# A transformer block on one core: three operations in another place in the rows of the loop, and the products of the last row spread anew over its slots

## The reference

```
xn  = (x - mean) / sqrt(var + 1e-5)
q,k,v = xn @ w_qkv.T + b_qkv                   # 16 heads of 32
att = softmax(q k.T / sqrt(32), causal) v
ffn = (silu(xn gate_w.T * gate_s) * (xn up_w.T * up_s)) @ down_w.T * down_s    # width 1408
out = x + att @ w_out.T + b_out + ffn
```

## Time and profile before

| | |
|---|---|
| median of 3 runs | 1941.37 us (1941.12 to 1942.3) |
| the profiled execution: its own time / its span in the trace | 1944.31 / 1942.6 us |
| PE busy | 1898.3 us, 98% |
| PE weight loads (beside PE) | 919.1 us, 47% |
| DVE / ACT / POOL busy | 1333.2 / 1294.1 / 1376.0 us (69 / 67 / 71%) |
| DMA packets | 840163, 267.93 MB |
| granted clock of TensorE, mean | 0.999 |

### The profile page before, as it was taken

The page is one execution under the profiler, slowest core; times in us unless marked ns, Lnnn a source line. Parts: engine busy times, 40 slices in busy tenths (PEclk is TensorE's granted clock), DMA queues, the critical chain, the costliest instruction groups (busy, mean ns, idle before and its releaser), DMA issues.

```text
span 1942.6 us, 48936 instructions
## 1 busy us (share of the span) xinstructions
PE 1898.3 (98%) x15875; PEld 919.1 (47%) x15875; DVE 1333.2 (69%) x3912; ACT 1294.1 (67%) x2315; POOL 1376.0 (71%) x1105
## 2 busy tenths in 40 slices
PE   5999999999999999999999999999999999999998
PEld 2444444444444444444444444444444444444443
DVE  8886766767666676766767666676766767667664
ACT  4876676666666676676766666676666766666574
POOL 1596687866678676687866778676687866778665
PEclk9999999999999999999999999999999999999999
DMA  9259777686876859777686876859678695876766
GB/s 341 47 93 161 145 121 150 116 152 130 151 144 110 160 104 162 137 122 150 115 153 129 152 145 109 158 103 166 135 122 148 114 156 126 150 147 112 132 131 120
DMA packets 840163, 267.93 MB, mean 138 GB/s; under 512 B 812976, under 2 KB 812976, under 8 KB 839344
## 3 DMA queue, kind: packets, MB, share of 16 engines
q1 hardware_dynamic: 839984, 265.15, 72.3%
HBM read 46.94 MB, written 16.78 MB: 33 GB/s over the span
## 4 chain that ended last, share of the span: by engine, by line
PE 72%; POOL 9%; issue 5%; DVE 5%; DMA 4%; SPq 3%; ACT 1%; DVEq 0%; POOLq 0%; ACTq 0%
PE ps L601 72%; POOL phl L1381 3%; POOL region_b L1338 3%; DMA p_t<-phl 3%; SPq L507 2%; DMA memory<-down 1%; POOL memory L1376 1%; DVE p L1268 1%; DVE memory L1059 1%; POOL rstd L1334 1%; SPq L587 1%; SPq L589 0%; DVE hidden_tmp L1201 0%; POOL region_a L1343 0%; POOL o_hl L1386 0%
## 5 line engine op out<-in xcount | busy, mean ns | idle before, releaser
L601 PE MATMUL ps<-x_t,memory 128*128 128x512 f16 x4376 | 994.8, 379 | 5.2 <-DVE qk L1151 2.0
L1381 POOL TENSOR_TENSOR phl<-p,phl 128x1024 f16<-128x1024 f32 x320 | 683.0, 2134 | 381.6 <-ACT phl L987 381.4
L977 ACT ACTIVATE p<-p,nmax 128x384 f32<-128x384 f32 (+3 forms) x1024 | 529.7, 557 | 275.9 <-DVE nmax L1268 256.7
L601 PEld LDWEIGHTS ps<-x_t,memory 128*128 128x128 f16 x4376 | 405.0, 97 | 494.0 <-issue 36.1
L1268 DVE CUSTOM_DVE_ANT_0 p<-ps,causal,cst 128x384 f32<-128x384 f32 (+3 forms) x1024 | 515.0, 546 | 98.2 <-PE ps L601 78.1
L987 ACT CAST phl<-p 128x1024 f16<-128x1024 f32 x320 | 334.1, 1044 | 40.1 <-DMA p_t<-phl 24.2
L601 PE MATMUL ps<-memory 128*128 128x512 f16 (+1 forms) x1705 | 340.5, 352 | 1.1 <-DVE bout_bc L1133 0.8
L1376 POOL TENSOR_TENSOR memory<-hidden_tmp,memory 128x512 f16<-128x512 f32 x176 | 205.0, 1165 | 70.4 <-ACT memory L949 70.4
L1276 DVE TENSOR_REDUCE ps<-ps 128x132 f32<-128x264 f32 (+1 forms) x320 | 122.0, 381 | 164.4 <-PE ps L601 164.3
L601 PEld LDWEIGHTS ps<-vv,p_t 128*128 128x128 f16 x5120 | 186.2, 96 | 92.6 <-issue 14.4
L601 PEld LDWEIGHTS ps<-memory 128*128 128x128 f16 (+1 forms) x1705 | 142.9, 100 | 159.6 <-issue 7.9
(11 more groups left out here) (81 smaller groups left out, 1319.1 us busy)
## 6 DMA issues: line engine op xcount, KB each, us to landing
region_b<-x SPq DMA_DIRECT2D x31, 1024.0 KB, 5.9
out<-region_b SPq DMA_DIRECT2D x64, 256.0 KB, 2.4
p_t<-phl SPq DMA_TRANSPOSE x640, 3.2
memory<-w_qkv SPq DMA_DIRECT2D x3, 1024.0 KB, 7.9
memory<-down SPq DMA_DIRECT2D x1, 2816.0 KB, 21.9
memory<-gate SPq DMA_DIRECT2D x1, 2560.0 KB, 9.5
memory<-up SPq DMA_DIRECT2D x1, 2560.0 KB, 15.3
region_a<-o_hl SPq DMA_TRANSPOSE x66, 3.3
```

Of the source, the lines that this page charges most:

```text
L601: return nc.tensor.matmul(o, lhsT=l, rhs=r, start=start, stop=stop, skip_group_check=True)
L977: last = nc.scalar.activation(cols, cols, ACT.Exp, scale=-1.0, bias=nmax[:, s % 2, i:i + 1])
L1381: g.tensor_tensor(phl[:, s % 2, 1, :], p32[:, s % 2, :], phl[:, s % 2, 0, :], ALU.subtract)\
```

## The change

Four edits, all of them of order; each product, each transfer and each vector operation is still there once.

1. SP, rows 1 to 14: `turn_x` moves from the head of slot 15 to between hi15 and lo15.
2. ACT, rows 1 to 14, slot 13: k3's high half goes ahead of g9's tanh.
3. POOL, rows 1 to 14, slot 12: `n2 n3` go from place 0 to place 1, behind p_lo of chunk 12.
4. Row 15 gets tables of its own. On PE its slots 9 to 13 hold 20 products instead of 24 (slot 12 keeps 24), and what is taken out goes to slots 15 to 19.

```
+PLAN_LAST = PLAN[:9] + [
+    "u4*2 g5*2 u5*1",
+    "u5*1 g6*2 u6*2", "g7*2 u7*2 g8*1", "q3*3 k3*3", "g8*1 u8*2 g9*2", "u9*2 g10*2", "u10*2 d0*2", "d0*2",
+    "d0*2 d1*1", "d1*2", "d1*3",
+]
...
-    "| | q3 u8 | x0 |", "g9 k3 | x1 | | |", "u9 g10 | x2 x3 | | u10 |", "| | | |", "| | | |", "| | | |",
+    "| | q3 u8 | x0 |", "k3 g9 | x1 | | |", "u9 g10 | x2 x3 | | u10 |", "| | | |", "| | | |", "| | | |",
...
-    "u5 | |", "u6 R0 n0 n1 | | u7", "n2 n3 | |", "u8 l0 | |", "u9 | u10 l1 |", "l2 l3 | |", "| |", "| |", "| |",
+    "u5 | |", "u6 R0 n0 n1 | | u7", "| n2 n3 |", "u8 l0 | |", "u9 | u10 l1 |", "l2 l3 | |", "| |", "| |", "| |",
...
-                    if s == (15 if prev else 13) and nxt:
+                    if s == 13 and not prev:
                         sp.wait_ge(sem["up_ready"], at(b, "up_ready", NT)).then_inc(wait_over["sp"], 1)
                         turn_x(b + 1)
...
                         sp.dma_start_transpose(p_t[:, i, 0, :, :], phl[:, i, 0, :]).then_inc(sem[name], 16)
+                        if s == 15 and prev and nxt:
+                            sp.wait_ge(sem["up_ready"], at(b, "up_ready", NT)).then_inc(wait_over["sp"], 1)
+                            turn_x(b + 1)
```

More of the change, by code:

```diff
@@ L82 @@
 ]
-PLAN_LAST = PLAN[:14] + ["u10*2 d0*2", "d0*2", "d0*2", "d1*2", "d1*2", "d1*2"]
+PLAN_LAST = PLAN[:9] + [
[3 more added lines that the diff above has]
+]
 PLAN_TAIL = ["D2*6 D3*1", "D3*5 o0*3", "o2*3 o3*3 o1*3"]
@@ L191 @@
 ]
-DVE_LAST = DVE_MID[:16] + ["| | |", "d0 | | |", "| | |", "| | | d1"]
-POOL_LAST = list(POOL_MID)
-POOL_LAST[10:14] = [text + f" c{t}" for t, text in enumerate(POOL_MID[10:14])]
+DVE_LAST = [
[3 rows of a table added]
+]
+ACT_LAST = [
[3 rows of a table added]
+]
+POOL_LAST = [
+    "| | b0 b1", "| | b2 b3", "| | f0 f1", "| | f2 f3", "u0 | |", "| |", "| | u1", "u2 | |", "u3 | |", "| | u4",
+    "u5 | | c0", "u6 | | u7 c1", "| | c2", "| | u8 c3", "| |", "u9 | u10 |", "| |", "| |", "| |", "| |",
+]
 DVE_TAIL = ["| | | D2", "| | | D3", "o0 o2 o3 o1 | | |"]
@@ L214 @@
     "first": dict(DVE=DVE_FIRST, ACT=ACT_FIRST, POOL=POOL_FIRST), "mid": dict(DVE=DVE_MID, ACT=ACT_MID, POOL=POOL_MID),
-    "last": dict(DVE=DVE_LAST, ACT=ACT_MID, POOL=POOL_LAST), "tail": dict(DVE=DVE_TAIL, ACT=ACT_TAIL, POOL=POOL_TAIL),
+    "last": dict(DVE=DVE_LAST, ACT=ACT_LAST, POOL=POOL_LAST), "tail": dict(DVE=DVE_TAIL, ACT=ACT_TAIL, POOL=POOL_TAIL),
 }
```

## The result

| | before | after |
|---|---|---|
| median of 4 runs | 1941.38 us | 1954.26 us (1953.16 to 1955.57) |
| ratio, 95% interval | | 1.0066, 1.0048 to 1.0083 |
| profiled execution: its own time / span | 1944.31 / 1942.6 us | 1954.83 / 1953.1 us |

The account below looks back on a forecast made before the run. PE was taken as the bound, busy 1898.3 of 1942.6 us. The loop's +16.8 - 6.5 = +10.3 and the last row's -2.7 gave +7.6 us, added to the median 1941.37: 1949.0 us, range 1941.5 to 1957.

Parts of the forecast that it names:

- r0's wait: Rows 1 to 14, slot 17: PE waits at r0 for later x_t transposes, 1.2 us a row, +16.8 us.
- The lost time taken away: Rows 1 to 14: today's losses at V12 and V15, 6.5 us in all, go away, -6.5 us.
- Edit 3, 1 us won alone: POOL, rows 1 to 14: p_lo of chunk 12 earlier, V12 never waits; by itself 1 us of the 6.5 won.
- edit 2, nothing: ACT, rows 1 to 14: k3's halves come earlier, nothing on PE waits for them, 0 us.
- lo15 hidden beneath r0: Rows 1 to 14: V15 follows r0 by 1.73 us of products, so lo15's landing costs no further wait.
- The last row: Row 15: 7.0 us to win, less 2.0 at u8, 1.0 at d0, 1.3 at V17 and V18; net -2.7 (0 to -6).
- u8's wait: Row 15: u8 needs g8's bank, so PE stands while tanh and `gated` run, +2.0 us.
- d0's: Row 15, slot 17: d0's fifth part waits for tile 10's low half from POOL, +1.0 us (0 to 1.5).
- (2): Rival, the queue keeps up: x_t block in 4 us or less, or faster landing, no r0 wait; 1932 us, chance 0.08.
- (3): Rival, the two halves cancel: shortest block, +8.9, and nearly all 7 us of the last row; 1943.8 us, chance 0.18.
- (4): Rival, the long block stays: stop tied to SP's third issue, 2.2 us a row, +21.6; 1963 us, chance 0.06.
- the check in the prediction's last part: New trace, rows 1 to 14: 14 x_t waits of about 1 us, none on p_t, x_t block 2.3 to 2.5 later.

Follow-up runs that it names:

- page_shift: The changed kernel with a never-taken branch in the loop body that makes PE's code 72 instructions longer: 1957.75 us, 1.0073 of the kernel before.
- sp_undone: The changed kernel with edit 1 undone, the x_t transposes again at the head of slot 15: 1946.40 us, 1.0019 of the kernel before.
- last_alone: The kernel before with only the last row's tables of the changed kernel (edit 4): 1939.55 us, 0.9981 of the kernel before.
- sp_alone: The kernel before with edit 1 alone, the x_t transposes between hi15 and lo15: 1961.52 us, 1.0096 of the kernel before.
- r0_late: The changed kernel with d3's first two parts ahead of V15 and r0 behind it in the loop: 1964.07 us, 1.0109 of the kernel before.

## Why the prediction was right, and where its sizes were off

The direction, the range and the mechanism hold: PE's wait moved from V15 to r0 and grew. The forecast was +7.6 us; measured were 12.9 in the medians, and 10.5 between the profiled executions that the sum was made for. Term by term, in those two executions:

- **r0's wait, 1.2 us a row, +16.8**: measured 19.9 us of idle time in 14 waits, 22.2 with the hidden part, 1.58 a row. This is the term that was mis-sized. The shift of the x_t block was foreseen as 2.4 us; against V0 it was 2.3 (80.78 instead of 78.48). But I took the block at its shortest, 5.52 us, because SP's third and fourth issue would come after the stop. They did, and the second ran into it: 1.88 us instead of 1.23. The block is 6.17 us on the mean, as in the kernel before (6.25). That is 0.65 more than I took; the other terms of a row's wait are off by 0.15 at most (r0 could start 0.13 earlier, by edit 2). The stop is bound to PE's place in its code and not to SP's, and SP is in the middle of its queue there in either order. page_shift bears it out: with the packet at 79.6 the block was as short as I took it, 5.55, but hi15 ahead of it was held up instead, and PE waited no less.
- **The lost time taken away, -6.5**: right for p_t, with 1.8 us more from the 0.13 us pause behind V11, which edit 2 removed and which I had not seen in the timeline. 22.2 - 6.4 - 1.8 is 14.0, and the rows show 13.9.
- **Edit 3, 1 us won alone; edit 2, nothing**: the first is wrong in sign. Alone it costs 2.6 us, and edits 2 and 3 together some 7 (sp_undone against last_alone). The prediction names the reason itself, that a row late at V12 finds V15's transposes landed, and still took 1 us of gain from it; that POOL's p_lo, and with it x_t and lo15, would come later (0.17 us at chunk 14) it had ruled out. In the changed kernel this cost does not arise, since the wait for x_t covers it; there the two edits bring V13 earlier, and with it hi15 and x_t, by 0.33 us (sp_alone). What they are worth depends on the order on SP, which a sum of terms taken one by one does not hold.
- **lo15 hidden beneath r0**: right, and r0_late shows its size, 1.2 us a row.
- **The last row, -2.7**: -4.0 in the trace, -3.4 by last_alone. What there was to win adds up to 7.3 us by its own terms (4.95, four times 0.16, and 1.7), not 7.0. u8's wait was 1.67 us for 2.0 foreseen, d0's 0.9 for 1.0; the third was foreseen at V17 and V18, 1.3 together, and came at V16, 1.0. The half clock is gone.
- **The rivals.** No block was under 5.5 us, so the queue did not keep up (2). The halves did not cancel (3). The long block (4) is the one that had a part: the block stayed long. But not for the reason given there, that the stop falls on SP's third issue: it was the second that was held up here; and it was not at its longest. The range holds the time because its upper end was reckoned with 1.6 us a row, which is what came (1.58), and not with the 1.2 that I took.

Of the check in the prediction's last part, the x_t block starts 2.3 us later (2.3 to 2.5 said), hi15 goes out 0.23 us behind V13's end, x_t's last landing follows its issue by 3.3 us.

## What to carry to other kernels

A queue that issues transfers in order is an engine like the others: before moving a group of transfers behind one more instruction, look what that instruction waits for, and which consumer of the group comes first, which here was not the one whose wait was being cured. A wait that is last in a chain may be paid for by an earlier one; removing the earlier one alone won nothing here, or lost. And what cured a full stretch of a queue was one of its transfers moved into a hole elsewhere, 12.5 us of difference to the kernel that lacks only this and 9.2 to the kernel before, 3.4 of them by the last row; permuting the stretch did not.

## What the runs showed of the hardware

A 16 KB packet of the instruction queue goes out some 10 times in a row of 116 us. The one that falls between lo14 and lo15 went ahead, in each of the 14 rows of the kernel before, of a stop of the transposes of 1.0 to 1.5 us. While they stand, SP's own issue is held (1.23 us became 1.9 to 2.3 where it fell on one issue alone), so the queue behind it moves as well. The place of the stop follows the count of PE's instructions: with 72 more of them in the loop body, never executed, the packet went out 2 to 3 us earlier in both kernels, and another issue was held. The kernel before was then 6.2 us slower, in part by the branch itself. So code that is not even executed changed the time of a kernel whose work was the same; how much of that is the packet's was not separated.
